# Reordering the front of a four-block graph network kernel: weight halves, checks, idle products, splits and a bias

## The reference, cut to what matters

```python
h = jnp.maximum(_layernorm(x), 0.0)
h0 = h @ W + b                                   # "the projection"
adj = zeros(N, N); adj[row, col] = 1; adj[col, row] = 1; adj += eye
adj = adj / jnp.maximum(adj.sum(axis=1, keepdims=True), 1.0)
out, cur = dw[0] * h0, h0
for i in range(3):                               # "the hops"
    cur = adj @ cur
    out = out + dw[i + 1] * cur
x = x + relu(out)
...
# block 2: messages by edge type, aggregation, two layer norms, FFN
# block 3: symmetric normalised adjacency; block 4: two SAGE layers
```

## Time and profile before

| | |
|---|---|
| median of three runs | 376.28 us (375.48 to 376.69) |
| profiled execution: own time | 376.17 us |
| profiled execution: span from first to last instruction | 373.7 us |
| TensorE busy (matmuls) | 364.9 us, 98% |
| VectorE, ScalarE, GpSimd busy | 172.8, 81.4, 57.9 us |
| mean granted TensorE clock | 0.990 |

### The profile page before, as it was taken

The page is one execution under the profiler, slowest core; times in us unless marked ns, Lnnn a source line. Parts: engine busy times, 40 slices in busy tenths (PEclk is TensorE's granted clock), DMA queues, the critical chain, the costliest instruction groups (busy, mean ns, idle before and its releaser), DMA issues.

```text
span 373.7 us, 3790 instructions
## 1 busy us (share of the span) xinstructions
PE 364.9 (98%) x1426; PEld 202.8 (54%) x1426; DVE 172.8 (46%) x326; ACT 81.4 (22%) x174; POOL 57.9 (15%) x48
## 2 busy tenths in 40 slices
PE   5999999998999999999999999999999999999996
PEld 2447889885444444444444457444455656446642
DVE  5698998998322122184032032006683628121210
ACT  3344664224200000000000003221242450221000
POOL 5000000005799000010100110001120172000000
PEclk9799999999999999999999999999999999999999
DMA  7100001249700000096000055057142000000011
GB/s 226 55 1 2 3 4 39 76 138 313 281 0 0 2 0 0 0 307 226 2 0 0 0 85 141 0 86 124 16 78 37 0 2 0 0 2 0 1 55 56
DMA packets 43809, 22.01 MB, mean 59 GB/s; under 512 B 35536, under 2 KB 36048, under 8 KB 43792
## 3 DMA queue, kind: packets, MB, share of 16 engines
q1 hardware_dynamic: 43264, 20.85, 20.1%
q0 software_dynamic: 240, 0.79, 0.7%
q10 hardware_dynamic: 288, 0.13, 0.1%
HBM read 20.72 MB, written 1.05 MB: 58 GB/s over the span
## 4 chain that ended last, share of the span: by engine, by line
PE 89%; DVE 7%; DMA 1%; ACT 1%; issue 0%; SPq 0%
PE bank L1150 42%; PE bank L1225 15%; PE bank L1344 7%; PE bank L1256 7%; PE bank L587 4%; PE bank L560 4%; PE bank L584 3%; PE bank L1138 2%; DVE h L991 2%; PE bank L576 2%; PE bank L521 2%; DVE lo L1009 1%; DMA x<-in_x 1%; DVE h L975 1%; DVE adj L971 1%; PE bank L543 1%
## 5 line engine op out<-in xcount | busy, mean ns | idle before, releaser
L1150 PE MATMUL bank<-slots,h_t 128*128 128x512 f32 x192 | 83.6, 592 | 0.8 <-ACT h_t L870 0.8
L1150 PEld LDWEIGHTS bank<-slots,h_t 128*128 128x128 f32 x192 | 35.9, 190 | 43.6 <-issue 43.6
L1225 PE MATMUL bank<-slots,wall 128*128 128x512 f32 x128 | 55.7, 593 | 0.0
L1225 PEld LDWEIGHTS bank<-slots,wall 128*128 128x128 f32 x128 | 24.0, 190 | 28.7 <-issue 28.7
L1031 DVE TENSOR_TENSOR slots<-bank,bias 128x512 f32<-128x512 f32 x16 | 11.1, 692 | 43.9 <-PE bank L1150 43.9
L1150 PE MATMUL bank<-wall,h_t 128*128 128x512 f32 x64 | 29.0, 593 | 0.5 <-ACT h_t L870 0.5
L1344 PE MATMUL bank<-wall,slots 128*128 128x512 f32 x64 | 28.4, 592 | 0.0
L1150 PE MATMUL bank<-h_t,slots 128*128 128x384 f32 (+2 forms) x96 | 28.0, 451 | 0.0
L1256 PE MATMUL bank<-slots 128*128 128x512 f32 x64 | 27.8, 592 | 0.0
L587 PE MATMUL bank<-slots 128*128 128x112 bf16 x256 | 27.8, 228 | 0.0
L584 PE MATMUL bank<-slots 128*128 128x140 bf16 x128 | 26.2, 242 | 0.1
(11 more groups left out here) (166 smaller groups left out, 444.6 us busy)
## 6 DMA issues: line engine op xcount, KB each, us to landing
slots<-in_L_gnn_W_rel SPq DMA_DIRECT2D x4, 1024.0 KB, 10.9
slots<-in_L_gnn_W_ffn SPq DMA_DIRECT2D x2, 2048.0 KB, 12.7
slots<-in_L_gnn_Wl SPq DMA_DIRECT2D x32, 64.0 KB, 2.4
slots<-in_L_gnn_Wr SPq DMA_DIRECT2D x32, 64.0 KB, 2.4
x<-in_x SPq DMA_DIRECT2D x4, 256.0 KB, 6.1
bias<-in_L_gnn_W SPq DMA_DIRECT2D x1, 1024.0 KB, 8.0
slots<-in_L_gnn_W_self SPq DMA_DIRECT2D x1, 1024.0 KB, 5.7
bias<-in_L_gnn_b_rel SPq DMA_DIRECT2D x4, 256.0 KB, 9.2
```

The source lines that it names most:

```text
L1150: ins = pe.matmul(bank, left, right, start=start and i == 0, stop=stop and i == len(pairs) - 1)
L1225: ins = pe.matmul(main[m][:], wall[:, r, s, tile(m)], msg[r][:, s, :], start=(r == 0 and s == 0), stop=(r == R - 1 and s == NT - 1))
```

## The change

- `w0` is loaded as two transfers of 512 KB with a semaphore each; the first is issued ahead of x tile 1, the second ahead of x tile 2. TensorE waits for the first ahead of the first projection product and for the second ahead of the third.
- On VectorE the checks move ahead of `moments(1)`, with `scale_and_shift(0)` in their middle; `moments(1)` goes behind the first of the split edge weights, `scale_and_shift(1)` two steps later.
- On ScalarE `normalise` is cut in a `root` and the rest. `root(0)` goes ahead of the copy of the keys; `empty(t)` goes between `normalise(t)` and `root(t + 1)`.
- Of TensorE's products of zeros, 10 and 6 behind the plan become 4 ahead of the transpose of the edge weights, 2 ahead of `fill_h(0)` and 3 behind it. In the first projection tile `fill_h(1)` stands behind the third product instead of the second.
- The four splits leave their place ahead of group 3: one goes between the last steps of the chunk stage, one to its end, two into `run_blocks` behind `symmetric(2)` and `symmetric(3)`. The sum of `dw` goes ahead of group 0, and the bias is scaled by ScalarE at the start of `run_blocks`.

The branch for unevenly sorted edges (`If_ne`) gets the same moves; it is not taken with these inputs.

```diff
-            sp.dma_start(w0, w0_in.rearrange("(k p) n -> p k n", p=P)).then_inc(w0_loaded, 16)
+            halves = w0_in.rearrange("(a k p) n -> a p k n", p=P, a=2)
+            sp.dma_start(w0[:, 0:KT // 2, :], halves[0]).then_inc(w0_loaded[0], 16)
             sp.dma_start(x[:, 1, :], x_in[P:2 * P, :]).then_inc(x_loaded[1], 16)
+            sp.dma_start(w0[:, KT // 2:KT, :], halves[1]).then_inc(w0_loaded[1], 16)
...
+            root(0)
+            act.wait_ge(keys_t_ready, 1)
+            act.activation(keys_t, keys_bank[:, 0:3 * P].rearrange("p (a c) -> p a c", a=3), ACT.Copy).then_inc(keys_out, 1)
             normalise(0)
+            empty(0)
+            root(1)
             normalise(1)
-            empty(0)
+            empty(1)
+            root(2)
             normalise(2)
-            empty(1)
+            empty(2)
+            root(3)
             normalise(3)
-            empty(2)
             keep_projection(0)
             empty(3)
...
             moments(0)
-            moments(1)
             dve.wait_ge(const_ready, 1)
             link(dve.tensor_reduce(check[:, 0:1], apart, AX.X, ALU.max),
...
+            scale_and_shift(0)
             link(dve.tensor_scalar(check[:, 3:4], check[:, 0:1], float(WIDE - 1), None, ALU.is_gt),
...
-            scale_and_shift(0)
...
             link(dve.tensor_tensor(rest[:, 0, :], wgt_t, parts[:, 0, :], ALU.subtract))
-            scale_and_shift(1)
+            moments(1)
             link(dve.tensor_copy(parts[:, 1, :], rest[:, 0, :]))
             link(dve.tensor_tensor(rest[:, 1, :], rest[:, 0, :], parts[:, 1, :], ALU.subtract))
+            scale_and_shift(1)
...
+                sum_steps()
...
-                    if g == RING:
-                        for m in range(NT):
-                            split_projection(m)
-                        weigh_bias()
                     hots(g)
...
                 keep_early_counts()
+                split_projection(0)
                 link(add_tails(NB // 4 * 3, 5, slice(R, OUT_R)))
...
                 keep_last_counts()
+                split_projection(1)
...
+            spin(4)
             pe.wait_ge(wgt_loaded, 16)
...
-            spin(10)
+            spin(2)
...
             fill_h(0)
-            spin(6)
-            pe.wait_ge(w0_loaded, 16)
+            spin(3)
             for m in range(NT):
                 pe.wait_ge(t_out, m + 1)
                 for k in range(KT):
+                    if m == 0 and k % (KT // 2) == 0:
+                        pe.wait_ge(w0_loaded[k // (KT // 2)], 16)
...
-                    if k == KT // 2 - 1 and m + 1 < NT:
+                    if k == (KT - 2 if m == 0 else KT // 2 - 1) and m + 1 < NT:
                         fill_h(m + 1)
...
+            act.wait_ge(steps_summed, 1)
+            act.wait_ge(b0_loaded, 16)
+            act.activation(b0[:], b0[:], ACT.Copy, scale=dw_sum[:]).then_inc(bias_weighed, 1)
...
-            for t in range(NT):
+            for t in range(2):
                 symmetric(t)
+            for t in range(2, NT):
+                symmetric(t)
+                split_projection(t)
...
+            dve.wait_ge(bias_weighed, 1)
             for m in range(NT):
                 weigh_projection(m)
```

More of the change, by code:

```diff
@@ L97, in gnn_program @@
         b0_loaded, dw_loaded, acc_ready = sem("b0_loaded"), sem("dw_loaded"), sem("acc_ready")
+        steps_summed = sem("steps_summed")
         built, early_kept, late_kept = sem("built"), sem("early_kept"), sem("late_kept")
@@ L102, in gnn_program @@
         tails, block_out = build_matrices(nc, sem, sb, block, wall, x, ident, ones, eye, eps, slow_flag, load_flag, banks, psum, slots, h, h_t,
-                       both_ways, bias, inv_cnt, hi[0], lo[0], ident_r, cnt_r, b0, dw, dw_sum, b0_loaded, dw_loaded, acc_ready, built, early_kept, late_kept,
+                       both_ways, bias, inv_cnt, hi[0], lo[0], ident_r, cnt_r, b0, dw, dw_sum, b0_loaded, dw_loaded, acc_ready, steps_summed, built, early_kept, late_kept,
                        proj_out, hi_ready, lo_ready, sym_ready, x_in, src_in, dst_in, typ_in, wgt_in, w0_in, b0_in)
         run_blocks(nc, sem, block, wall, tails, late_kept, block_out, x, ident, ones, eye, eps, load_flag, psum, slots, h, h_t, adj, cnt_r, both_ways, bias,
-                   inv_cnt, hi, lo, b0, dw, dw_loaded, acc_ready, built, proj_out, hi_ready, lo_ready, sym_ready,
+                   inv_cnt, hi, lo, b0, dw, dw_sum, b0_loaded, dw_loaded, acc_ready, steps_summed, built, proj_out, hi_ready, lo_ready, sym_ready,
                    dw_in, wself_in, bself_in, wrel_in, brel_in,
@@ L112, in build_matrices @@
 def build_matrices(nc, sem, sb, block, wall, x, ident, ones, eye, eps, slow_flag, load_flag, banks, psum, slots, h, h_t,
-                   both_ways, bias, inv_cnt, hi0, lo0, ident_r, cnt_r, b0, dw, dw_sum, b0_loaded, dw_loaded, acc_ready, built, early_kept, late_kept,
+                   both_ways, bias, inv_cnt, hi0, lo0, ident_r, cnt_r, b0, dw, dw_sum, b0_loaded, dw_loaded, acc_ready, steps_summed, built, early_kept, late_kept,
                    proj_out, hi_ready, lo_ready, sym_ready, x_in, src_in, dst_in, typ_in, wgt_in, w0_in, b0_in):
@@ L162, in build_matrices @@
         x_loaded = [sem(f"x{t}_loaded") for t in range(NT)]
-        w0_loaded = sem("w0_loaded")
+        w0_loaded = [sem(f"w0{half}_loaded") for half in range(2)]
         const_set, ident_ready, const_ready = sem("const_set"), sem("ident_ready"), sem("const_ready")
@@ L247, in keep_projection, with root, normalise @@
                 act.activation(h[:, m, :], proj_bank[m], ACT.Copy).then_inc(proj_out, 1)
-            def normalise(t):
+            def root(t):
                 act.wait_ge(var_ready, t + 1)
                 act.activation(std[:, t:t + 1], mean_var[:, t, 1:2], ACT.Sqrt, bias=eps[:]).then_inc(std_ready, 1)
+            def normalise(t):
                 act.wait_ge(shift_ready, t + 1)
@@ L424, in keep_last_counts, with sum_steps @@
                 dve.tensor_copy(cnt_r[:, :, N - DB + TAIL:N], lower[:, :, TAIL:DB]).then_inc(late_kept, 1)
-            def weigh_bias():
+            def sum_steps():
                 dve.wait_ge(dw_loaded, 16)
-                dve.wait_ge(b0_loaded, 16)
-                link(dve.tensor_reduce(dw_sum[:], dw[:], AX.X, ALU.add))
-                link(dve.tensor_scalar(b0[:], b0[:], dw_sum[:], None, ALU.mult))
+                dve.tensor_reduce(dw_sum[:], dw[:], AX.X, ALU.add).then_inc(steps_summed, 1)
             def split_projection(m):
@@ L505, in _ @@
                     dve.tensor_copy(wall[:, R, t, :], psum[NT + t]).then_inc(slow_cnt_out, 1)
-                for m in range(NT):
+                for m in range(2):
                     split_projection(m)
-                weigh_bias()
+                dve.wait_ge(proj_out, NT)
+                sum_steps()
                 link(dve.memset(tails, 0.0))
@@ L673, in run_blocks @@
 def run_blocks(nc, sem, block, wall, tails, late_kept, block_out, x, ident, ones, eye, eps, load_flag, psum, slots, h, h_t, adj, cnt_r, both_ways, bias,
-               inv_cnt, hi, lo, b0, dw, dw_loaded, acc_ready, built, proj_out, hi_ready, lo_ready, sym_ready, dw_in, wself_in, bself_in, wrel_in, brel_in,
+               inv_cnt, hi, lo, b0, dw, dw_sum, b0_loaded, dw_loaded, acc_ready, steps_summed, built, proj_out, hi_ready, lo_ready, sym_ready, dw_in, wself_in, bself_in, wrel_in, brel_in,
                g1_in, be1_in, g2_in, be2_in, wf1_in, bf1_in, wf2_in, bf2_in, w2_in, b2_in,
@@ L746, in run_blocks @@
         inv_root_ready, inv_cnt_ready = sem("inv_root_ready"), sem("inv_cnt_ready")
-        hop_ready = sem("hop_ready")
+        hop_ready, bias_weighed = sem("hop_ready"), sem("bias_weighed")
         self_ready, self_out, msg_ready, msg_out, agg_ready, agg_out = (
@@ L972, in symmetric, with split_projection @@
                                          accum_out=row_sum[:, t:t + 1]).then_inc(adj_ready, 1)
+            def split_projection(m):
+                dve.wait_ge(proj_out, m + 1)
+                dve.tensor_tensor(lo[0][:, m, :], h[:, m, :], hi[0][:, m, :].bitcast(F32), ALU.subtract).then_inc(lo_ready, 1)
             def weigh_projection(m):
                 dve.scalar_tensor_tensor(h[:, m, :], h[:, m, :], dw[:, 0:1], b0[:], ALU.mult, ALU.add).then_inc(acc_ready, 1)
-            for t in range(NT):
+            for t in range(2):
                 symmetric(t)
+            for t in range(2, NT):
+                symmetric(t)
+                split_projection(t)
             dve.wait_ge(adj_ready, NT)
```

2 lines of the change are left out of this document (removed).

## The result

The changed kernel takes 370.73 us (median of 4 runs, 370.53 to 370.87) beside 375.88 us of the kernel before (4 runs, 375.09 to 376.69). The ratio is 0.9862, with a 95% interval from 0.9838 to 0.9886: faster by 1.4%, or 5.15 us. The forecast was 371.4, faster. The profiled execution took 370.67 us, with a span of 368.6 where before had 373.7.

What follows compares the result with a forecast made beforehand. It took TensorE's products of zeros ahead of the projection to bound the front, and VectorE the hops; -6.3 (to chunk stage end) + 1.2 (hops) + 0.2 (register reads) = -4.9 against 376.28 gave 371.4 us, range 370.6 to 374.8.

Steps and rivals of the forecast that it cites:

- Checks: VectorE's checks ahead of `moments(1)`: 1.25 us earlier, 0.32 lost to `scale_and_shift(0)`, ready at 7.08 instead of 8.01.
- Plan products: TensorE's plan products behind the checks: 0.51 us at full clock instead of 1.02, done at 7.59.
- Products of zeros: TensorE ahead of the projection: four hidden, clock kept up, projection starts at 9.25 instead of 15.69, 6.4 us earlier.
- Weights: Loads of `w0` and x tile 1: all three in time, the last by 0.4 us.
- Projection: TensorE's projection ends at 24.3 us; register reads of chunk offsets cost 0.2, bounds 0 and 0.86.
- VectorE: Group 0 starts at 16.7, 2.3 us earlier; splits and bias off the path save 4.08, together 6.4.
- the signs at the prediction's end: Expected trace: clock 1.00 from 7 to 15 us, TensorE without gaps in the chunk stage, which ends near 55.4.
- End of the chunk stage: Two splits fall into VectorE's idle 0.86 and 0.80 us and cost nothing; gain up to here 6.3.
- Hops: Two splits of 0.60 us each on VectorE's chain cost 1.2, bounds 0 and 1.25; ScalarE's bias is hidden.
- Rival A: TensorE's clock falls all the same at 7.7 us: 374.4, or 372.6 if it rises earlier; chance 0.25.
- Rival B: Loads come late, x tile 1 and the weights' second half; tile 1 at 10.6 gives 373.5 us; chance 0.08.
- Rivals C and D: C: clock falls and stays down longer, 378.1 us, chance 0.05; D: VectorE's group 0 starts late, 375.4 us, chance 0.07.

Runs made afterwards that it cites:

- the last experiment: Changed kernel without `spin(2)` and with all four projection splits on GpSimd, started behind VectorE's copy of the late counts (`late_kept`): 370.10 us, ratio 0.9871.
- first experiment: Kernel before with only the products of zeros placed as in the changed one (4, 2 and 3 instead of 10 and 6): 372.40 us, ratio 0.9907.
- the first of those experiments: Changed kernel with the four projection splits on GpSimd, each as soon as its projection tile is copied: 374.01 us, ratio 0.9957.

## Why the prediction was right

Its sum was -6.3 + 1.2 + 0.2 = -4.9. The trace has -6.22 up to the end of the chunk stage and +1.07 behind it, -5.15. By its own steps:

- *Checks* and *Plan products*: ready at 6.98 (forecast 7.08), plan done at 7.59 (7.59). Right. With the weights ahead of tile 1 this step is indispensable, as the kernel with VectorE's old order shows; what it brings alone no run shows.
- *Products of zeros*: the projection starts at 9.17 (9.25), right. ScalarE's copy starts 0.03 behind the transposes (8.49, 8.52); the earlier trace rows had 0.04, not the 0.15 of the sum. That "TensorE is busy there is what could keep the clock up" was half right: without the four products the clock stayed up in three of four executions. Whether the four products add certainty, as the fourth execution suggests, four runs can't settle.
- *Weights*: the landings were forecast between 6.1 and 8.35 for the first half, at about 8.35 for x tile 1 and at 10.6 for the second half. They came at 2.12 + 3.8 = 5.9, 2.59 + 5.3 = 7.9 and 3.10 + 6.1 = 9.2. That the second half came 1.4 before the whole had is within what loads vary by: it landed between 9.2 and 10.0 in the traces with halves, the whole between 9.5 and 11.0 in three. No step hung on it.
- *Projection*: 15.41 long instead of 15.05. The gaps are not those of register reads, since ScalarE's copies release the weight loads in both. In tile 0, 0.27 us are lost in its first six products (2.84 instead of 6 x 0.43), whose first weight load can start only at 9.17, behind ScalarE's copy (before, it stood ready ahead of the product), and 0.09 in tile 1, behind the wait of 0.65. The forecast had 0.2 for something else; that it was near is luck. ScalarE's starts were right: tile 1 at 10.36 (10.4).
- *VectorE*: group 0 at 16.80 (16.7), right. That "VectorE sets the later groups" is not what the trace shows: TensorE sets them, without a gap, as the signs at the prediction's end had it. The comparison of 4.45 with 3.86 us a group leaves out the ring of three buffers, which lets VectorE's lead shrink over the groups before TensorE has to wait. What followed from it was right all the same: a gain on one engine only would have been lost. With the splits back TensorE waits 2.1 us for VectorE, and with ScalarE's old order VectorE waits 3.10 for TensorE.
- *End of the chunk stage*: 55.44 (55.4), adjacency at 57.45 (57.4). Two splits were free, as forecast: in the last experiment VectorE has none of them, and the adjacency starts at 57.19, waiting for TensorE, against 57.32 in the kernel without `spin(2)` that has both: at most 0.13.
- *Hops*: 1.07 instead of 1.2. The last split is partly free: with the splits back, 0.12 us pass between the last adjacency instruction and the next, for the accumulator's read, and the split lies over that.
- *Sum*: 5.1 us of span. The time outside the span is 2.07 us where it was 2.47, which no step spoke of. It differs by kernel: 2.3 to 3.4 us in the 54 executions of before, 1.9 to 2.1 in the changed kernel. What lies in it no trace shows. So the measured 370.73 is 0.7 under the forecast: 0.25 from the terms above and 0.4 from outside the span. It lies at the low end of the stated range (370.6; by its own terms, 0.2 and 0.5 under the forecast, that end is 370.7).

Rival A did not occur in any of 4 executions of the changed kernel, but its mechanism is real: it shows in the kernel with VectorE's old order. Rival B's opposite came true in the profiled execution. Rivals C and D found nothing: group 0 was not late, and even without any product of zeros behind the keys' transposes no execution was slower than the median of before.

What the prediction did not see is the spread. The kernel before, 54 executions beside the experiments, has four kinds: 7 with a mean granted clock of 0.989 to 0.991 and spans of 373.5 to 374.3; 21 with 0.994 or 0.995 and 371.6 to 372.7; 21 with 0.998 or more and 372.9 to 373.6; 5 with 0.998 or more and 370.0 to 371.0. The profiled one, which I argued from (0.990, 373.7), is of the first kind. The 48 executions of the changed kernel and of eight of the experiments (all but the two without `spin(4)` and the two with VectorE's or ScalarE's old order) are never below 0.998. So a good part of the gain is that a bad case no longer occurs: the best of before (370.0) lies 1.4 us above the changed kernel's span. Why before has two kinds at the full mean clock, 3 us apart, stays open: only executions with their traces would tell, and there is none of those two. One candidate is an opening at half rate that lasts longer, since the record shows 1.00 in that opening too (last section); no run tests it.

## What to carry to other kernels

Products of zeros that are meant to keep TensorE's clock up are insurance and are judged by the spread of many executions, not by one trace; here the other means was to shorten the idle stretch itself (from 2.15 to 0.67 us), by moving what waits for a transfer behind what doesn't. When two engines feed each other through a ring and are nearly level, as VectorE and TensorE are here, forecast both and take the later, and look at which of them waits: undone one at a time, the edits of the front cost from nothing to the whole gain, so such prices can't be added. Before giving work to an idle GpSimd, look at every VectorE instruction beside it, small ones too: what reads and writes SBUF alone can stand still until GpSimd's instruction ends (1.0 us here).

## What the hardware showed that I had not expected

GpSimd holds VectorE up for much of the time that it works: in the first of those experiments splits of 6.66 us (1.29 + 3.48 + 1.89; the same four take 5.03 in the last one) cost VectorE 4.3, in the last one an instruction on four numbers a partition waits 1.0 us for their end. VectorE's adjacency instructions, which read one operand from PSUM and one from SBUF, are untouched (0.69 us, and all four runs). By the Trainium skill, page "SBUF — State Buffer", section "Who interferes with whom", the two engines share a pair of ports that one of them holds for a whole instruction, and VectorE needs it with two inputs from SBUF, or in the fast modes of copies and of operations with a scalar. The runs agree in each kind seen here (comparisons, products and an addition of two SBUF tensors, a copy, a scaling); in which mode the copy and the scaling ran, no run shows.

The landing of a load differs between executions by more than splitting it brings: the second half of the weights landed between 9.2 us (changed kernel) and 10.0 (without `spin(4)`), the whole at 9.5 (first experiment), 10.6 and 11.0 (weights in one transfer).

The granted clock is shown as 1.00 from the start of the execution, although TensorE's opening runs at half rate: its products of zeros (128x512) start 0.43 us apart there, and 0.21 apart later. Only the durations tell. The opening ends at different times: in the kernel before and the changed one the three transposes at 5.23 are already 0.12 us apart, in seven of the experiments they are still 0.22 apart, and in one of these half rate lasts to about 7.1 us. A mean granted clock of 1.0 is therefore no proof of full rate.
